# A GNN layer with residual and layer norm: wider row groups, 40 KB rows in a four-slot ring, another opening and another last group

## The reference

```python
agg = adj @ (x @ W_agg)
h = w[:, None] * relu(agg) + (1.0 - w)[:, None] * x
out = layernorm(x + h, axis=-1)      # eps 1e-5, over 64 columns
```

## Time and profile before

| | us |
|---|---|
| median of 3 runs | 653.8 |
| span of the profiled execution | 651.5 |
| TensorE matmul busy | 496.9 (76%) |
| TensorE weight loads busy | 174.3 |
| VectorE busy | 58.3 |
| ScalarE busy | 31.4 |
| bytes moved by DMA | 272.84 MB, 419 GB/s over the span |

### The profile page before, as it was taken

One profiled execution on the slowest core, in us unless ns is written; L12 is line 12 of the kernel. 1 busy time (PEld: TensorE's weight loads), 2 busy tenths in 40 slices (PEclk: granted clock), 3 DMA queues, 4 the chain that ended last, 5 costly groups with the idle time before them and its releaser, 6 DMA issues.

```text
span 651.5 us, 5854 instructions
## 1 busy us (share of the span) xinstructions
PE 496.9 (76%) x2496; PEld 174.3 (27%) x2496; DVE 58.3 (9%) x107; ACT 31.4 (5%) x41; POOL 0.7 (0%) x7
## 2 busy tenths in 40 slices
PE   6999887677777778767777777877777777777775
PEld 5733222222222122222222212212222221222245
DVE  1300012000210003000030000300003000030021
ACT  2200010000100001000020000200002000100000
POOL 0000000000000000000000000000000000000000
PEclk9999999999999999999999999999999999999999
DMA  8999999999999999999999999999999999999994
GB/s 316 433 427 428 430 424 431 432 423 433 430 426 432 425 430 433 424 431 431 425 433 423 431 433 424 428 434 426 432 424 432 432 424 432 426 425 428 422 429 164
DMA packets 21481, 272.84 MB, mean 419 GB/s; under 512 B 2656, under 2 KB 2912, under 8 KB 4576
## 3 DMA queue, kind: packets, MB, share of 16 engines
q1 hardware_dynamic: 20032, 270.57, 97.8%
q10 hardware_dynamic: 1440, 2.13, 0.9%
HBM read 270.60 MB, written 2.10 MB: 419 GB/s over the span
## 4 chain that ended last, share of the span: by engine, by line
DMA 80%; PE 18%; issue 0%; DVE 0%; ACT 0%; SPq 0%; ACTq 0%; DVEq 0%
DMA ring<-adj_main_dram 65%; PE acc L184 15%; DMA ring<-adj_mid_dram 9%; DMA ring<-adj_last_dram 5%; PE xw_ps L172 2%; PE xT_ps L156 1%; DMA xres<-x_dram 1%; ACT L225 0%; SPq L120 0%; ACT xT L225 0%; DVE xw L258 0%; ACTq L220 0%; PE rows_ps L194 0%; ACT std L233 0%; DVE y L279 0%
## 5 line engine op out<-in xcount | busy, mean ns | idle before, releaser
L184 PE MATMUL acc<-ring,xw 128*64 128x512 f32 (+2 forms) x2304 | 468.4, 552 | 137.3 <-DMA ring<-adj_main_dram 119.6
L184 PEld LDWEIGHTS acc<-ring,xw 128*64 128x64 f32 x2304 | 151.0, 137 | 449.2 <-issue 217.9
L275 DVE SCALAR_TENSOR_TENSOR y<-rows_ps,w_sb 128x512 f32<-128x512 f32 (+2 forms) x9 | 5.7, 632 | 560.3 <-PE rows_ps L194 560.3
L231 ACT COPY aggT<-acc 128x512 f32<-128x512 f32 (+2 forms) x9 | 4.8, 538 | 550.8 <-PE acc L184 550.8
L172 PE MATMUL xw_ps<-wagg,xT 64*128 64x64 f32 x128 | 15.5, 424 | 0.7 <-ACT xT L225 0.7
L172 PEld LDWEIGHTS xw_ps<-wagg,xT 64*128 64x128 f32 x128 | 14.2, 326 | 3.1 <-issue 2.0
L156 PE MATMUL xT_ps<-ident,xres 128*128 128x128 f32 x32 | 8.9, 433 | 5.3 <-DMA xres<-x_dram 4.8
L194 PE MATMUL rows_ps<-ident,aggT 128*128 128x128 f32 x32 | 5.4, 288 | 6.3 <-ACT aggT L231 6.3
L231 ACT ACT_TABLE_LOAD x7 | 9.0, 1283 | 11.5 <-DVE xres L290 11.4
L233 ACT ACT_TABLE_LOAD x7 | 9.0, 1283 | 0.1
L258 DVE COPY xw<-xw_ps 128x256 f32<-128x256 f32 x16 | 6.0, 419 | 24.4 <-PE xw_ps L172 24.4
(11 more groups left out here) (11 smaller groups left out, 6.9 us busy)
## 6 DMA issues: line engine op xcount, KB each, us to landing
ring<-adj_main_dram SPq DMA_DIRECT2D x112, 2048.0 KB, 35.3
ring<-adj_mid_dram SPq DMA_DIRECT2D x16, 1536.0 KB, 27.5
ring<-adj_last_dram SPq DMA_DIRECT2D x3, 2048.0 KB, 29.0
xres<-x_dram SPq DMA_DIRECT2D x4, 512.0 KB, 6.3
out_dram<-xres ACTq DMA_DIRECT2D x7, 256.0 KB, 9.4
ring<-adj_last_dram SPq DMA_DIRECT2D x1, 1024.0 KB, 29.5
ring<-adj_last_dram SPq DMA_DIRECT2D x2, 512.0 KB, 25.8
out_dram<-xres ACTq DMA_DIRECT2D x1, 192.0 KB, 7.8
```

The costliest lines, as they stand in the source:

```text
L184: last = nc.tensor.matmul(acc[h * D:(h + 1) * D, 0:width], xw[:, j], ring[:, slot, at:at + width], start=j == 0, stop=j == T - 1)
L231: nc.scalar.copy(aggT[:, 0:width], acc[:, 0:width]).then_inc(agg_copied, 1)
L275: step(nc.vector.scalar_tensor_tensor(out=v, in0=rows_ps[:, 0:n * D].rearrange("p (n d) -> p n d", d=D), scalar=0.0, in1=over_row(w_sb[:, ...
```

## The change

- Six groups of ten row tiles in place of seven of eight, then one group of three, then one of one (`MAIN_SLOTS`, `MID_SLOTS`, `LAST_SLOTS`). A main load has eight steps j: 40 KB for each partition, 5 MB in all, eight loads a group, through four slots (`SUB`, `RING`). A main group takes two PSUM banks, 320 columns of each; for each j there are four matmuls of 320 columns.
- The middle group is loaded in nine loads (`MID_LOADS`), seven of eight steps (12 KB for each partition) and then five and three. The last group has ten loads that become smaller (`LAST_LOADS`), all into one slot, with a semaphore each; they need that slot and no other. In these two groups the even steps j sum into rows 0 to 63 and the odd ones into rows 64 to 127, and a matmul with two stacked identities (`ident2`) turns the result back and adds the halves. TensorE turns the middle group back behind the first load of the last group.
- The opening: `x` in one transfer on SP; `w_agg` and `w` on ScalarE's queue; ScalarE's table loaded ahead of its first copy. All PSUM tensors are slices of one tensor `bank`.
- relu of the main groups on ScalarE, as it copies `acc`; the residual x(2-w) for all tiles once, ahead of the groups, in place of two steps in each. Seven counted VectorE steps a group in place of nine.
- The last group's mean and variance by `bn_stats` and `bn_aggr`, and its last step as one tensor_scalar.

```diff
-HALVES = 2
-MAIN_SLOTS = 8
-MID_SLOTS = 6
-LAST_SLOTS = 2
-SUB = 4
-LAST_LOADS = (16, 16, 16, 8, 4, 4)
-RING = 8
-X_PARTS = 4
+HALVES = 1
+MAIN_SLOTS = 10
+MID_SLOTS = 3
+LAST_SLOTS = 1
+SUB = 8
+RING = 4
+MID_LOADS = (8, 8, 8, 8, 8, 8, 8, 5, 3)
+LAST_LOADS = (16, 13, 10, 7, 5, 4, 3, 2, 2, 2)
...
-            for i in range(X_PARTS):
-                part = slice(i * T // X_PARTS, (i + 1) * T // X_PARTS)
-                sp.dma_start(xres[:, part], x.rearrange("(p t) d -> p t d", p=P)[:, part]).then_inc(x_in[i], 16)
-                if i == 0:
-                    sp.dma_start(wagg2[0:D, :], w_agg).then_inc(wagg_in, 16)
-                    sp.dma_start(wagg2[D:P, :], w_agg).then_inc(wagg_in, 16)
+            sp.dma_start(xres[:], x.rearrange("(p t) d -> p t d", p=P)).then_inc(x_in, 16)
...
+            j = 0
+            for i, n in enumerate(MID_LOADS):
+                load = MID_LOAD0 + i
                 sp.wait_ge(slot_free, load - RING + 1)
...
+                sp.dma_start(ring[:, load % RING, 0:n * MID_SLOTS * P],
+                             adj_mid[j // SUB, :, j % SUB:j % SUB + n].rearrange("q s n -> q (s n)")
+                             ).then_inc(loaded[load % RING], 16)
+                j += n
+
+            sp.wait_ge(slot_free, LAST_LOAD0 - RING + 1)
             j = 0
...
+            for k, n in enumerate(LAST_LOADS):
+                sp.dma_start(ring[:, LAST_LOAD0 % RING, j * P:(j + n) * P],
+                             adj_last[:, j:j + n].rearrange("q s n -> q (s n)")).then_inc(last_loaded[k], 16)
                 j += n
...
+            def contract(slot, j0):
+                for s in range(SUB):
                     j = j0 + s
...
+                    for b in range(BANKS):
+                        for h in range(2):
+                            at = s * COLS + (h * BANKS + b) * CHUNK
+                            last = nc.tensor.matmul(acc[h * D:(h + 1) * D, b, 0:CHUNK], xw[:, j], ring[:, slot, at:at + CHUNK],
+                                                    start=j == 0, stop=j == T - 1)
                 last.then_inc(slot_free, 1)
...
             j = 0
...
+            for k, n in enumerate(LAST_LOADS):
+                pe.wait_ge(last_loaded[k], 16)
+                for s in range(n):
+                    h = (j + s) % 2
+                    last = nc.tensor.matmul(last_acc[h * D:(h + 1) * D, 0:P], xw[:, j + s],
+                                            ring[:, LAST_LOAD0 % RING, (j + s) * P:(j + s + 1) * P],
+                                            start=j + s < 2, stop=j + s >= T - 2)
                 j += n
...
+                if k == 0:
+
+                    pe.wait_ge(ident2_ready, 1)
+                    pe.wait_ge(agg_copied, MID + 1)
+                    pe.wait_ge(dve_step, MID * DVE_GROUP + DVE_PRE)
+                    for i in range(MID_SLOTS):
+                        turned = nc.tensor.matmul(rows_ps[:, i * D:(i + 1) * D], aggT[:, i * P:(i + 1) * P], ident2[:],
+                                                  start=True, stop=True)
+                    turned.then_inc(rows_done, 1)
...
+            for h in range(2):
+                act.dma_start(wagg2[h * D:(h + 1) * D, :], w_agg).then_inc(wagg_in, 16)
             act.dma_start(w_sb[:], w.rearrange("(p t) -> p t", p=P)).then_inc(w_in, 16)
+
+            nc.scalar.preload_act_table_set("sqrt_and_others")
...
+            v, t = y[:, 0], LAST_T0
+            dve.wait_ge(rows_done, LAST + 1)
+            step(nc.vector.tensor_scalar(v, rows_ps[:, 0:D], 0.0, w_sb[:, t:t + 1], ALU.max, ALU.mult), LAST_STEP0 + 1)
+            step(nc.vector.tensor_tensor(v, v, xres[:, t], ALU.add), LAST_STEP0 + 2)
+            step(nc.vector.bn_stats(stats[:], v), LAST_STEP0 + 3)
+            step(nc.vector.bn_aggr(mv[:], stats[:]), LAST_STEP0 + LAST_VAR_STEP)
+            dve.wait_ge(std_ready, LAST + 1)
+            step(nc.vector.reciprocal(rstd[:, 0:1], std[:, 0:1]), LAST_STEP0 + 5)
+            nc.vector.tensor_scalar(xres[:, t], v, mv[:, 0:1], rstd[:, 0:1], ALU.subtract, ALU.mult).then_inc(out_ready, 1)
```

More of the change, by code:

```diff
@@ L39, in gnn_residual_layernorm @@
     COLS = MAIN_SLOTS * P
[L40 to L48, removed]
+    HALF = MAIN_SLOTS // 2
+    BANKS = 2
+    CHUNK = HALF * P // BANKS
+    MID_BANKS = -(-MID_SLOTS * P // 512)
+    MID_CHUNK = MID_SLOTS * P // MID_BANKS
+    BLOCKS = T // 2 // PB
+    MID_LOAD0 = G * C
+    LAST_LOAD0 = MID_LOAD0 + len(MID_LOADS)
+    assert C * SUB == T == sum(MID_LOADS) == sum(LAST_LOADS) and LAST_T0 + LAST_SLOTS == T and C % RING == 0
+    DVE_PRE = 2
+    DVE_GROUP, VAR_STEP = 7, 6
+    LAST_STEP0 = DVE_PRE + LAST * DVE_GROUP
+    LAST_VAR_STEP = 4
     def arrivals(load):
@@ L175, in _, with turn_back @@
             pe.wait_ge(xw_copied, BLOCKS)
-            def contract(slot, j0, n_j, n_slots):
-                width = n_slots // HALVES * P
-                for s in range(n_j):
+            def contract(slot, j0):
+                for s in range(SUB):
                     j = j0 + s
[L182 to L185, removed]
+                    for b in range(BANKS):
[3 more added lines that the diff above has]
+                                                    start=j == 0, stop=j == T - 1)
                 last.then_inc(slot_free, 1)
-            def turn_back(g, n_slots):
+            def turn_back(g):
                 pe.wait_ge(agg_copied, g + 1)
                 pe.wait_ge(dve_step, g * DVE_GROUP + DVE_PRE)
-                for k in range(n_slots // HALVES):
+                for k in range(HALF):
                     last = nc.tensor.transpose(rows_ps[:, k * P:(k + 1) * P], aggT[:, k * P:(k + 1) * P], ident[:])
@@ L214, in _ @@
-            turn_back(LAST, LAST_SLOTS)
+                    contract(c % RING, c * SUB)
+                turn_back(g)
+            j = 0
+            for i, n in enumerate(MID_LOADS):
+                load = MID_LOAD0 + i
+                pe.wait_ge(loaded[load % RING], arrivals(load))
+                for s in range(n):
+                    h = (j + s) % 2
+                    for b in range(MID_BANKS):
+                        at = s * MID_SLOTS * P + b * MID_CHUNK
+                        last = nc.tensor.matmul(mid_acc[h * D:(h + 1) * D, b, 0:MID_CHUNK], xw[:, j + s],
+                                                ring[:, load % RING, at:at + MID_CHUNK], start=j + s < 2, stop=j + s >= T - 2)
+                last.then_inc(slot_free, 1)
+                j += n
@@ L294, in _ @@
-            group(MID, MID_T0, MID_SLOTS)
-            group(LAST, LAST_T0, LAST_SLOTS)
+                base = g * DVE_GROUP + DVE_PRE
+                dve.wait_ge(rows_done, g + 1)
+                for h in range(2):
+                    slots = bass.ds(g * MAIN_SLOTS + h * HALF, HALF)
+                    last = nc.vector.tensor_tensor(
+                        y[:, h * HALF:(h + 1) * HALF],
+                        rows_ps[:, 0:MAIN_SLOTS * D].rearrange("p (k h d) -> p h k d", h=2, d=D)[:, h],
+                        over_row(w_sb[:, slots]), ALU.mult)
@@ new lines, in _ @@
+                step(last, base + 1)
+                normalise(g, g * MAIN_SLOTS, MAIN_SLOTS, base)
+            base = MID * DVE_GROUP + DVE_PRE
+            dve.wait_ge(rows_done, MID + 1)
+            step(nc.vector.scalar_tensor_tensor(out=y[:, 0:MID_SLOTS],
+                                                in0=rows_ps[:, 0:MID_SLOTS * D].rearrange("p (n d) -> p n d", d=D),
+                                                scalar=0.0, in1=over_row(w_sb[:, MID_T0:LAST_T0]),
+                                                op0=ALU.max, op1=ALU.mult), base + 1)
```

122 lines of the change are left out of this document (57 added, 65 removed).

## The result

The changed kernel takes 649.24 us (median of 5 runs, 648.10 to 652.22) against 653.91 for the kernel before: a ratio of 0.9937, 95% interval 0.9915 to 0.9958. That is 4.7 us less; 5.8 us less was forecast (648.0), and the range held. The runs of before differ by 0.3 us, those of the changed kernel by 4.1 us, which the forecast had no word for. The profiled execution is one of the longer ones, 651.25 us; its span is 649.4 us against 651.5 before.

A forecast was written before the change was run, and what follows sets the result against it. DMA transfers set the pace, TensorE waits. Pace -4.2, opening -0.9, change of groups +0.6, lag -0.6, finish -1.0 make -6.1, taken as -5.8 for instruction fetches: 653.8 to 648.0 us, range 645.0 to 652.2.

The forecast's parts named there:

- the term for the opening: At the start, one transfer of x with ring loads right behind it closes gaps: 0.9 us less, ends 0 and 1.7.
- Pace of the transfers: All loads: fewer, longer loads save 70 fixed parts of 0.06 us, 4.2 us less, ends 1.4 and 7.0.
- the long rows bring nothing: Rival on the loads' pace: each byte costs the same as before, so 652.2 us; chance 0.14.
- the cover: At the start, TensorE's later arrival at adj, about 32.6 us, costs nothing, since queued transfers leave 13 us in hand.
- From the main to the middle group: At this change of groups the queue waits briefly for released slots: 0.6 us more, ends 0 and 2.0.
- enough until T + 11.1: Three queued middle loads of 3.69 us keep transfers going until 11.1 us after T, the last main load's landing.
- The clock rival: TensorE's clock falls while idle before main loads; the last main load ends about 2.5 us later, 650.5 us; chance 0.11.
- the forecast's case: The whole kernel: the terms hold as summed, 648.0 us; chance 0.58.
- Behind the last byte: At the end: TensorE finishes nearer the last landing, 0.6 us less, and the chain after the last matmul shortens, 1.0 less.
- the forecast's stretch: From the last main load's landing T through the last group: T + 40.7, or 41.1 us with copy and turn.
- The slower rival: TensorE's loop outgrows its instruction buffer and is fetched again, 664 us if one DMA engine carries it; chance 0.07.
- the lag: At the end, TensorE finishes 0.8 us behind the last landing instead of about 1.4: 0.6 us less, ends 0 and 1.0.

The follow-up runs named there:

- the half loads: The changed kernel with SUB = 4 and RING = 8, so 20 KB rows and eight slots of half the size: 647.16 us.
- first experiment: The changed kernel with w_agg and w issued by SP between x and the first ring load, not on ScalarE's queue: 647.27 us.
- the last experiment: The 643.25 us kernel (w_agg and w on SP, middle loads of 16, 16, 16, 8, 8 steps, unread matmuls between main loads) without those matmuls: 643.33 us.
- the kernel with the extra matmuls: The changed kernel with six matmuls of 320 columns, never read, behind each main load but a group's last: 647.43 us.

## Why the prediction was right, and where it was not

The sign and the size held, the size in part by luck: the term for the opening was too small, and two prices were missing or too small, that of the late `w` and that of the change of groups.

- **Pace of the transfers: right.** 12.125 us a load was measured, 12.14 is what 10 x 1.207 + 0.066 gives. The bytes of the 48 main loads take 582.0 us; in 120 loads of 2 MB at the pace of before they would take 587.3. That is 5.3 less for the main groups' bytes, where 4.2 was forecast for everything: I had rounded the fixed part down to 0.06, and the half loads give 0.073. The rival that the long rows bring nothing is refuted. The Trainium skill's three cycles a packet (DMA: Bandwidth & Descriptors, Why small descriptors are slow) would make an estimated 0.03 us a load; the measured 0.066 to 0.073, completion included, are more than twice that.
- **Opening: the cover was wrong.** The step that failed is "I cost that at nothing ... the cover is 13 us". I moved `w` and `w_agg` to another queue and priced only the issue that left ScalarE, not what they would stand behind. They stood behind 40 KB rows; TensorE came 12.2 us late, its first load took 11.6 us and not the 8.8 of the forecast, and the ring ran dry: 2.0 us (first experiment). The term for the transfers themselves, 0.9, measured 2.7 (x in one transfer). Together 0.7 less. The Trainium skill had the mechanism, in DMA: Bandwidth & Descriptors, section Queues, rings and completion order: each engine takes turns between its queues, a packet at a time. The landings of `w` (7.0, 16.9, 25.2 us) agree with the turns, and it speaks against this part of the change. By the Trainium skill's section a turn drains a packet of typically 9 to 17 descriptors; here a turn was one row, since about eight long rows went by while the eight rows of `w` did.
- **From the main to the middle group: right place, wrong size.** I had 0.6 us, ends 0 and 2.0. With the clock full it is 3.3 (44.5 against 41.2). The step that failed reads "enough until T + 11.1": in the changed kernel the rate falls 8.5 us behind T already, from 418 GB/s to 172 in the microsecond from 606, 61 in the next and 0 from 608 to 610. T is the landing of the slowest engine, and the others run ahead: the first rows of the middle group start 2 us before the last row of the last main load ends. Behind the empty stretch the rate needs more than ten us to recover (418 GB/s from 625 on).
- **The clock rival came true along with the forecast's case.** It was given 0.11 and 2.5 us at the last main load. The clock falls in most of the 3.3 us gaps (mean 0.936), and at the last main load it costs 3.0 where it falls there (47.5 against 44.5). That it costs nothing elsewhere in the main groups was foreseen and is shown by the last experiment. The Trainium skill's rule (TensorE: Matmul & The Clock Gate, HAM oscillation) holds in this trace in part: by the Trainium skill every burst starts at half clock, here about every other one does. I should have read it as likely, priced by its place. This rival is also where most of the spread comes from: the kernel with the extra matmuls has a fifth of it. TensorE's 8.8 us for a load at full clock were right (8.83), though the terms given for them add up to 8.95.
- **Behind the last byte.** The last matmul ends 0.5 us behind the last landing (644.15 to 644.66), less than forecast, since the gap had let TensorE catch up; without the gap TensorE bounds the end, and the forecast's stretch is met to 0.1 us. The finish became 0.9 us shorter (1.0 forecast); undone, it costs 1.1.
- **The loop stays in the instruction buffer.** The queue of the fetches shows as many as in the earlier trace rows:

```profile
q8 instruction: 7, 0.11, 0.1%
```

The slower rival is refuted, as is the Trainium skill's sentence of a buffer of two blocks (Runtime: NRT & Kernel Launch, Instruction fetch mechanics); its 2048 instructions for TensorE agree.

The terms as measured: 5.3 less for the pace, 2.7 for the opening, 0.9 for the finish and 0.9 for the lag; 2.0 more for the small rows, 3.3 more at the change of groups, up to 3.0 more for the clock there. That is 4.5 less with the last load fast and 1.5 with it slow. The median is 4.7 below before, the span of the profiled execution 2.1. The opening, 1.8 us better than forecast, and the small rows, 2.0 us worse, cancelled by luck, so that the total was nearer than its parts.

## What to carry to other kernels

A ring holds time, not slots: when loads become shorter at a change of stage, add up what the slots then hold and compare it with the release of the next one plus the way to its first bytes, with two us in hand for engines that run ahead (11.0 us were too little here, 13.8 enough). A small transfer that someone waits for goes ahead of the large ones in their own queue, not beside long rows in another. A loss that is read from one profile comes off the time of that execution, not off the median. An idle gap on a hidden engine may lower its clock at no cost, until one of its bursts happens to release something that is short.

## What the runs showed of the hardware

- After the queue has been empty the transfers are slower than the engines' busy share says: 332 GB/s at a share of 0.88 and 379 at 1.00 (613 to 621 us), where 425 goes with 1.01 just ahead of the gap. Why they restart slowly is open.
- In the changed kernel 15 of the 17 main loads behind an idle gap of 3.3 us or more start slowly, and 5 of the 24 behind a shorter one (those five had 1.6 to 2.5 us). With the extra matmuls, where most gaps are 1.7 us, four loads of the main groups start slowly.
- Two queues take turns on a DMA engine row by row: 16 rows of 256 bytes for each engine had landed 27.2 us after the start beside rows of 16 and 40 KB, and 9.0 us after it beside rows of 4 KB.
- Of the last main load the 16 engines end up to 2 us apart.
- Rows of 40 KB move at the pace that rows of 12 and 16 KB give when it is drawn out in a straight line, to 0.1%.
